# Last layer's hops as float32 64x64 quarter products instead of float32r products over a block matrix

## The reference, cut to what matters

```python
# X = relu(layernorm(x)), [128, 64, 512]; A = adj, [128, 64, 64]
Xw = X @ Wv + bv
sj = Xw @ aw[:d, 0]
si = Xw @ aw[d:, 0]
e = leaky_relu(sj[:, None, :] + si[:, :, None] + ab[0], 0.2)
alpha_matrix = A * exp(e)
transition = alpha_matrix / (sum(alpha_matrix, axis=-1) + 1e-12)
H = 0
Xk = X
for k in range(3):
    H = H + Xk @ Wk[k] + bk[k]
    Xk = einsum('bij,bjd->bid', transition, Xk)
out = x + relu(H)
```

## Time and profile before

| | before |
|---|---|
| median of 3 runs | 2319.44 us |
| lowest and highest | 2314.83 and 2321.06 us |
| span of the profiled execution | 2310.2 us |
| TensorE busy | 2287.1 us (99% of the span) |
| VectorE, ScalarE, GpSimd busy | 57%, 32%, 30% |
| granted TensorE clock, mean | 0.998 |

### The profile page before, as it was taken

One profiled execution on the slowest core, in us unless ns is written; L12 is line 12 of the kernel. 1 busy time (PEld: TensorE's weight loads), 2 busy tenths in 40 slices (PEclk: granted clock), 3 DMA queues, 4 the chain that ended last, 5 costly groups with the idle time before them and its releaser, 6 DMA issues.

```text
span 2310.2 us, 39569 instructions
## 1 busy us (share of the span) xinstructions
PE 2287.1 (99%) x16015; PEld 1860.6 (81%) x16015; DVE 1318.4 (57%) x2745; ACT 747.8 (32%) x1333; POOL 700.2 (30%) x930
## 2 busy tenths in 40 slices
PE   8999999999999999999999999999999999999998
PEld 5788788888878877888888888888778888888887
DVE  3565565656556555545554445555686757676753
ACT  3332323333233333333333333333433232323221
POOL 2433333343333322233322223332342121212120
PEclk9999999999999999999999999999999999999999
DMA  6323333333333343222232222222353333333330
GB/s 198 77 76 95 109 101 83 93 91 87 95 108 105 97 124 105 61 60 67 80 93 60 60 61 60 72 85 95 95 142 94 98 94 97 95 97 96 96 78 37
DMA packets 173479, 209.01 MB, mean 90 GB/s; under 512 B 64800, under 2 KB 81264, under 8 KB 173296
## 3 DMA queue, kind: packets, MB, share of 16 engines
q1 hardware_dynamic: 173296, 206.48, 32.0%
HBM read 88.91 MB, written 50.37 MB: 60 GB/s over the span
## 4 chain that ended last, share of the span: by engine, by line
PE 93%; DVE 2%; SPq 2%; ACT 1%; issue 1%; DMA 1%; POOL 0%; DVEq 0%; ACTq 0%
PE bank L327 50%; PE bank L317 29%; PE bank L588 4%; PE bank L343 3%; SPq L1406 2%; PE bank L528 1%; PE bank L501 1%; PE bank L307 1%; PE bank L378 1%; PE bank L511 1%; PE bank L294 0%; DVE hs L648 0%; DVE yt L961 0%; ACT g1T L1022 0%; PE bank L409 0%
## 5 line engine op out<-in xcount | busy, mean ns | idle before, releaser
L327 PE MATMUL bank<-w_hi,h3T_hi 128*128 128x512 f32 x768 | 302.4, 394 | 0.0
L327 PE MATMUL bank<-w_hi,h3T_lo 128*128 128x512 f32 x768 | 299.5, 390 | 0.0
L327 PE MATMUL bank<-w_lo,h3T_hi 128*128 128x512 f32 x768 | 299.5, 390 | 0.0
L615 DVE TENSOR_TENSOR Z_lo<-bank,Z_hi 128x512 fp32r<-128x512 f32 x128 | 87.1, 682 | 181.6 <-ACT Z_hi L973 181.3
L987 ACT ACTIVATE hn<-x,stA 128x512 f32<-128x512 f32 x192 | 140.7, 804 | 99.3 <-POOL stA L1214 99.3
L327 PEld LDWEIGHTS bank<-w_hi,h3T_hi 128*128 128x128 f32 x768 | 144.6, 188 | 30.2
L327 PEld LDWEIGHTS bank<-w_lo,h3T_hi 128*128 128x128 f32 x768 | 144.4, 188 | 30.2
L327 PEld LDWEIGHTS bank<-w_hi,h3T_lo 128*128 128x128 f32 x768 | 144.4, 188 | 30.2
L973 ACT ACTIVATE Z_hi<-bank 128x512 fp32r<-128x512 f32 x128 | 76.1, 596 | 251.1 <-PE bank L327 159.6
L1209 POOL TENSOR_SCALAR stA<-stA 128x4 f32<-128x4 f32 x48 | 11.5, 241 | 448.1 <-DVE stA L629 446.9
L615 DVE TENSOR_TENSOR cT_lo<-bank,cT_hi 128x256 fp32r<-128x256 f32 x128 | 44.7, 409 | 179.7 <-ACT cT_hi L973 179.7
(11 more groups left out here) (222 smaller groups left out, 5824.9 us busy)
## 6 DMA issues: line engine op xcount, KB each, us to landing
hGA<-hs SPq DMA_DIRECT2D x768, 64.0 KB, 2.0
mid<-x SPq DMA_DIRECT2D x32, 1024.0 KB, 4.8
x<-mid SPq DMA_DIRECT2D x32, 1024.0 KB, 5.8
x<-in_x SPq DMA_DIRECT2D x16, 1024.0 KB, 5.7
hGB<-hs SPq DMA_DIRECT2D x256, 64.0 KB, 2.0
out<-x SPq DMA_DIRECT2D x16, 1024.0 KB, 5.4
blk<-in_adj SPq DMA_DIRECT2D x128, 64.0 KB
adj<-in_adj SPq DMA_DIRECT2D x64, 64.0 KB, 3.3
```

What stands on the lines that cost most here:

```text
L327: ins = eng.matmul(b[:], h[l][:, k, ts], W[r][:, k, :], start=(k == 0 and i == 0), stop=(last and k == 3 and i == 2))
L615: return eng.tensor_tensor(lo, src, hi.bitcast(F), ALU.subtract)
```

## The change

Each hop is made of eight float32 products of a 64x64 matrix by 64x512, in two rounds of four. The four of a round use the four quarters of the array. T is no longer a block matrix with hi and lo parts: GpSimd writes it whole as "own" (a graph's matrix on its own half of the partitions), and ScalarE copies the half that the crossed quarters need to the other half of the partitions ("other"). Z is plain float32; ScalarE copies each bank in two halves of 64 partitions, both to the half of partitions t // 2. VectorE's lo parts of Z and T, GpSimd's four clearings of T, and the tile tt are gone. All four tiles of z1 (and of y) are opened first, and the hops of all four follow behind them; before, each tile had its hop at once. The last group is stored tile by tile. The allocations keep the other tiles' places (pads not shown).

```diff
-        T = [{"hi": alloc(pc, f"Thi{i}", [128, 4, 128], R), "lo": alloc(pc, f"Tlo{i}", [128, 4, 128], R)} for i in range(2)]
+        T = [{"own": alloc(pc, f"Town{i}", [128, 4, 64]), "other": alloc(pc, f"Tother{i}", [128, 2, 64])} for i in range(2)]
...
-            def l3_hop(b, full, g, t, zi):
-                pe.wait_ge(v_tlo, 2 * g + 2)
-                pe.wait_ge(v_zlo[zi], 4 * g + t + 1)
-                for i, (l, r) in enumerate(PASSES):
-                    ins = eng.matmul(b[:], T[g % 2][l][:, t, :], Z[zi][r][:, t, :], start=False, stop=(i == 2))
-                ins.then_inc(full, 1)
+            def l3_hop(zi, name, g):
...
+                pe.wait_ge(a_ts, 2 * g + 2)
+                pe.wait_ge(a_zh[zi], 8 * g + 8)
+                for r in range(2):
+                    for p, c in ((0, 0), (1, 1), (0, 1), (1, 0)):
+                        t = 2 * p + r
+                        b, h = bank.of((name, g, t)), HALF[p]
+                        left = T[g % 2]["own"][h, t, :] if p == c else T[g % 2]["other"][h, r, :]
+                        ins = eng.matmul(b[HALF[c], :], left, Z[zi][h, 2 * r + c, :], start=False, stop=True)
+                        if p != c:
+                            ins.then_inc(bank.done((name, g, t))[0], 1)
...
                 for t in range(4):
-                    b, full, _ = gemm_open(("z1", g, t), hT3[i], t, W3[1], (v_zlo[1], 4 * g + t + 1), False)
-                    l3_hop(b, full, g, t, 0)
+                    gemm_open(("z1", g, t), hT3[i], t, W3[1], (a_zh[1], 8 * g + 2 * t + 2), False)
+                l3_hop(0, "z1", g)
                 pe.wait_ge(p_wlo, lo_pool["w0"])
                 for t in range(4):
-                    b, full, _ = gemm_open(("y", g, t), hT3[i], t, W3[0], (v_y, 4 * g + t + 1), False)
-                    l3_hop(b, full, g, t, 1)
+                    gemm_open(("y", g, t), hT3[i], t, W3[0], (v_y, 4 * g + t + 1), False)
                     if t == 1 + (g == 0) and g + 1 < NG:
                         l3_rowsum(g + 1)
+                l3_hop(1, "y", g)
...
-            def l3_thi(g):
+            def l3_T_other(g):
                 act.wait_ge(p_tt, g + 1)
...
+                for p in range(2):
+                    copy(T[g % 2]["other"][HALF[p], :, :], T[g % 2]["own"][HALF[1 - p], 2 * p:2 * p + 2, :]).then_inc(a_ts, 1)
+
+            def l3_z(zi, key, g, t):
                 act.wait_ge(*bank.done(key))
                 if g:
-                    act.wait_ge(*bank.done((("z1", "y")[zi], g - 1, 3)))
-                copy(Z[zi]["hi"][:, t, :], bank.of(key)[:]).then_inc(a_zhi[zi], 1)
+                    for u in (1, 3):
+                        act.wait_ge(*bank.done((("z1", "y")[zi], g - 1, u)))
+                b = bank.of(key)
+                for c in range(2):
+                    copy(Z[zi][HALF[t // 2], 2 * (t % 2) + c, :], b[HALF[c], :]).then_inc(a_zh[zi], 1)
...
-                    pool.wait_ge(*bank.done(("qk", g, 3)))
-                    for tl in T:
-                        for n in ("hi", "lo"):
-                            eng.memset(tl[n][:].bitcast(F), 0.0).then_inc(p_zero3, 1)
...
+            last = kA(3, NG - 1)
+            for t in range(4):
+                sp.wait_ge(v_x4, 4 * NG - 3 + t)
+                eng.dma_start(out_v[NG - 1][:, t, :], xs[x_slot(last)][:, t, :]).then_inc(d_o[last % 4], 16)
```

More of the change, by code:

```diff
@@ L139, in build @@
             "x_bias q2 k2 z2 zmax zsub zexp2 zrec pn pt vv ct_hi ct_lo x3")
[L141 to L144, removed]
+        (v_dotA, v_sc, v_zc, v_lr, a_ee, p_al, v_rs, p_tt, a_ts, v_y, v_x4) = sems(
+            "dotA scol zc lrelu ee al rs T_own T_other y x4")
+        a_zh = sems("z0_halves z1_halves")
         ident = alloc(root, "ident", [128, 128])
@@ L232, in build @@
         bones = alloc(pc, "bones", [128, 128])
-        tt = alloc(pc, "ttt", [128, 4, 64])
-        alloc(pc, "pad5", [128, 128])
+        alloc(pc, "pad5", [128, 384])
         hT3.append(pair(pc, "h3T1"))
-        Z.append(pair(pc, "Z1"))
+        Z.append(alloc(pc, "Z1", [128, 4, 512]))
+        alloc(pc, "pad9", [128, 2048])
         bkb = alloc(pc, "bkb", [128, 3, 512])
@@ L902, in l3_rowsum @@
                 eng.reciprocal(rs[:], rs[:]).then_inc(v_rs, 1)
[L904 to L911, removed]
-            for g in range(NG):
[L914 to L920, removed]
+            for g in range(NG):
+                if g == 0:
+                    l3_rowsum(0)
+                    l3_sums(dve, eng, 1, (2, 3))
                 if g + 2 < NG:
                     stats_A(3, g + 2)
[L923 to L929, removed]
+                    if g == 0:
+                        adj_T(3, 1)
+                        l3_alpha(1)
+                    transposes(3, g + 2)
                 if g and g + 1 < NG:
@@ L1163, in act_program @@
                         copy(ptc[r][:].rearrange("p m n -> p (m n)"), bank.of(("pT", g, r))[:]).then_inc(a_pt, 1)
-            def l3_thi(g):
+            def l3_T_other(g):
                 act.wait_ge(p_tt, g + 1)
-                act.wait_ge(p_zero3, 4)
                 if g >= 2:
                     act.wait_ge(*bank.done(("y", g - 2, 3)))
-                for h in HALF:
-                    copy(T[g % 2]["hi"][h, :, h], tt[h, :, :]).then_inc(a_thi, 1)
-            def l3_zhi(zi, key, g, t):
+                    act.wait_ge(*bank.done(("y", g - 2, 1)))
+                for p in range(2):
+                    copy(T[g % 2]["other"][HALF[p], :, :], T[g % 2]["own"][HALF[1 - p], 2 * p:2 * p + 2, :]).then_inc(a_ts, 1)
+            def l3_z(zi, key, g, t):
                 act.wait_ge(*bank.done(key))
                 if g:
-                    act.wait_ge(*bank.done((("z1", "y")[zi], g - 1, 3)))
-                copy(Z[zi]["hi"][:, t, :], bank.of(key)[:]).then_inc(a_zhi[zi], 1)
+                    for u in (1, 3):
[3 more added lines that the diff above has]
+                    copy(Z[zi][HALF[t // 2], 2 * (t % 2) + c, :], b[HALF[c], :]).then_inc(a_zh[zi], 1)
             split_in_place(W3[0], d_w0)
@@ L1322, in l3_rowsum @@
                 pool.wait_ge(v_rs, 2 * g + 2)
-                pool.wait_ge(v_tlo, 2 * g)
-                eng.tensor_tensor(tt[:], al[:], rs[:], ALU.mult).then_inc(p_tt, 1)
+                if g >= 2:
+                    pool.wait_ge(*bank.done(("y", g - 2, 3)))
+                    pool.wait_ge(*bank.done(("y", g - 2, 1)))
+                eng.tensor_tensor(T[g % 2]["own"][:], al[:], rs[:], ALU.mult).then_inc(p_tt, 1)
             split_in_place(W3[1], "w1")
@@ L1553, in sp_program @@
                 gather(3, g + 2)
-                sp.wait_ge(v_x4, 4 * g + 4)
-                store_x(kA(3, g), out_v[g])
+                if g + 1 < NG:
+                    sp.wait_ge(v_x4, 4 * g + 4)
+                    store_x(kA(3, g), out_v[g])
+            last = kA(3, NG - 1)
+            for t in range(4):
+                sp.wait_ge(v_x4, 4 * NG - 3 + t)
+                eng.dma_start(out_v[NG - 1][:, t, :], xs[x_slot(last)][:, t, :]).then_inc(d_o[last % 4], 16)
             for i in range(4):
-                sp.wait_ge(d_o[i], 16 * len([k for k in range(3 * NG) if k % 4 == i]))
+                sp.wait_ge(d_o[i], 16 * len([k for k in range(3 * NG) if k % 4 == i]) + (48 if i == last % 4 else 0))
         block = root.enter_context(nc.Block())
```

18 lines of the change are left out of this document (9 added, 9 removed).

## The result

The changed kernel takes 2388.01 us (2387.45 to 2391.89, four runs), the kernel before 2319.03 us (2314.83 to 2321.06, four runs): a ratio of 1.0309 [1.0297, 1.0321], slower. The profiled execution spans 2390.1 us against 2310.2, 79.9 us more; by the medians it is 69.0 us more. The prediction was +41.6, a median of 2361 in a range of 2336 to 2382: the side and the mechanism came, the size did not, and the time lies above the range.

What follows compares the result with a forecast made beforehand. TensorE was taken to set the last layer's pace. Hops -19.8, first hop -4.0, row-sum waits +48.4, clock +14.4, end +2.6 made +41.6 us: span 2351.8, median 2361, range 2336 to 2382.

Steps and rivals of the forecast that it cites:

- Hops: Last layer's hops on TensorE: 2.72 us each before, 2.10 as quarter products; 32 hops save 19.8 us.
- The first hop: TensorE's wait for T's lo part and the low clock behind it both go: 4.0 us saved.
- The place and the cause of the new wait: TensorE stops at the row sum for alpha, because y tiles released together delay the fourth to S+10.8 (S: group's z2 start).
- The size of the wait: At the row sum: exponential at S+31.6, wait 3.5 us, bounds 2.7 (ScalarE's own path) and 4.7; 48.4 us in all.
- the sums' way: SyncE's DMA: 15.2 us from the store to issuing the sums in, landing 4.2 later, at S+30.2.
- Two waits of the fourteen: Row-sum waits by group: none in the first, 3.5 us in groups 1 to 13, 2.9 in group 14.
- The clock: Half clock behind the row-sum waits: nine falls of fourteen at 1.6 us each, 14.4 us; bounds none and 23.8.
- VectorE's and GpSimd's old work: Removing VectorE's lo parts and GpSimd's clearings gives nothing, as TensorE does not wait for them elsewhere.
- The end: From TensorE's last product to the end, last group stored by tiles: 8.9 us instead of 6.25, 2.6 more.
- Span and median: Median of the runs lies 9.2 us above the profiled span, left unchanged: span 2351.8, median 2361.
- Rival 2: Row-sum waits come and the clock falls in each: 2370 us, or 2387 with waits of 4.7; chance 0.22.
- The rule on copies of PSUM: PSUM copies may become the limit; ScalarE takes all Z copies, some 17 us of a 40 us group: delay, not capacity.

Runs made afterwards that it cites:

- experiment 7: Kernel before with its float32r hops behind all four tiles and the row sum behind the fourth y product: 2319.38 us, ratio 1.0021.
- experiment 1: Changed kernel with TensorE's row sum for the next group behind the fourth y product instead of the second: 2292.86 us, ratio 0.9912.
- 6: Changed kernel with the row sum behind the fourth y product and the last group stored whole instead of by tiles: 2297.21 us, ratio 0.9923.
- experiment 3: Kernel before with only its float32r hops moved behind all four tiles of z1 or y: 2414.53 us, ratio 1.0433.
- Experiment 2: Changed kernel with 20 overwritten products of 128x512 ahead of each row sum from group 2's on: 2359.7 us, ratio 1.0199.
- Experiment 4: Changed kernel with VectorE's sums for group g+2 ahead of the y tiles instead of between them: 2357.24 us, ratio 1.0189.
- experiment 5: Changed kernel with the row sum behind the fourth y product and four GpSimd clearings into unused memory put back: 2291.64 us, ratio 0.9907.
- experiment 8: Changed kernel, VectorE's g+2 sums first, VectorE copying z1 tiles 2 and 3 and making alpha before its transposes, norm_A later: 2300.62 us, ratio 0.994.

## Why the prediction was right in kind and short in size

**Hops, right.** Predicted 0.62 us each, 19.8 in all. The timeline gives 2.72 - 2.09 = 0.63, the spans of experiments 7 and 1 give 18.8 for all hops, the medians of 7 and 6 up to 23.

**The first hop, right.** The wait for the lo part of T, 2.3 us, is gone, and with it the low clock behind it.

**The place and the cause of the new wait, right.** It stands at the row sum and waits for alpha; experiment 1 removes it by one line, experiment 3 makes it with the old form. The delay starts where the prediction put it, with four y tiles that come free at once and the fourth done at S+10.8. So the change of placement is what makes the kernel slower, and not the quarters, which are a gain.

**The size of the wait, the first term that failed.** The step was: "The exponential starts at about S+31.6 ... a wait of 3.5 us." In groups 2 to 13 it came at S+33.0 on average and the waits were 3.5 to 6.2, 4.8 on average. The term that was mis-sized is the sums' way: out and back in were put at 15.2 us from the store to the issue of the sums in and 4.2 for their landing, from one group of before and a median; in the group read they took 16.0 and 4.6, and the median landing of the changed kernel is 4.9. The path through x and ScalarE was well sized: the last copy ends at S+30.7 to S+31.5, where the prediction had S+31.7.

One group was thin ground for such a term: in groups 2 to 13 of the kernel before, the time from the issue of the sums out to that of the sums in goes from 10.1 to 13.6 us (11.0 on average, 10.8 in the group taken). In the changed kernel the same step takes 11.5 us on average, in experiments 1 and 2 it takes 10.7 and the landing 4.2, and there the exponential starts at S+31.5 and S+31.7. So the prediction's sum came true for this chain in two of its neighbours; in the changed kernel the sums' way is some 1.4 us longer. Why, is open: that TensorE stops in every group is not enough, since in experiment 3, where it does too, the step takes 10.6 and the landing 4.1. Experiment 4 takes the sums off the path and leaves 2.9 us, near the floor of 2.7.

**Two waits of the fourteen were wrong.** Group 1 was put down like the rest and had 8.5 us: its x was issued at 1734.96 and its first statistics came only 14.5 us later:

```profile
1749.48 0.69 DVE L637 BATCH_NORM_STATS2 stA<-x 128x6 f32<-128x512 f32 x1 [13.49 <-DMA x<-mid]
```

Group 14 had 0.9 instead of 2.9, and group 0, put at nothing, had 0.8. In sum 67.5 us stand against 48.4: 19 us of the shortfall, of which the twelve groups with 4.8 instead of 3.5 make 15. What held up group 1's load was not found. The gathers issued just ahead of it do not explain it: in the kernel before they end 2.1 us ahead of this group's store (here 5.1) and the statistics start 9.1 us behind the store (here 14.9), and here the DMA engines move nothing any more in the last 5 us ahead of them:

```profile
1745.00:1750.00 5.00, 5.00 (x30) 2.86 (x29) 0.52 (x1) 2.37 (x4) 0.00 (x0) 1.00 0.00 0
```

Experiments 1 and 2 have the same delay (13.1 and 13.6 us), experiment 4 does not (8.4).

**The clock, the second term that failed.** The step was: "I take nine of fourteen, at 1.6 us each." All 13 long waits were followed by the lower level, at 2.26 us in the group read and 2.4 on average, 31 us together, against 14.4. The average comes from the distance of the row sums: twelve groups, from 1761.62 to 2296.97, take 535.35 us; a group of experiment 1, without a wait, takes 37.27 (1984.87 to 2022.14), twelve of them 447.2; the twelve waits take 57.3 and 12 x 0.16 more; 28.9 are left. Experiment 2 has 25 to 30 for its twelve. Both parts of the term were short, the count (nine instead of 13) and the price (1.6 instead of 2.4). The page TensorE: Matmul & The Clock Gate of the Trainium skill (HAM oscillation) describes a loop that goes cold in every pass because TensorE waits in every pass; here the trace agrees, 13 of 13. The size of one fall was taken from a single window of before in which the low clock lasted 3.4 us; here it lasted from the row sum at 2072.66 to 2077.09.

**VectorE's and GpSimd's old work.** "VectorE's lo parts and GpSimd's clearings cost nothing today and give nothing" was wrong in one place: without the clearings the wait for VV is 2.1 us longer, since GpSimd's h3T_lo then lies beside the steps that make VV (experiment 5).

**The end.** 8.9 us were predicted behind TensorE's last product and 7.1 came: the landing of 256 KB was taken at 4.2 us, the sums' time, and takes 2.0. Before it was 6.25: 0.85 more instead of 2.6.

**Span and median.** The prediction left 9.2 us between them as they were. It was no constant, and what the device does around the instructions is 1.8 us of it at most: the profiled execution of the changed kernel took 2391.89 us, 1.8 above its span, and so it is in every execution on record that lists its span (1.75 to 1.87). The rest was the spread between executions. The prediction of the median was 7 us too high for that, which hid a part of the miss: 38.3 us by the spans (2351.8 to 2390.1), 27 by the medians (2361 to 2388.0).

The account of the span: hops -19.8, first hop -4.0, waits at the row sum +67.5 and 15 x 0.16 = +2.4, clock +31.2 (13 x 2.4), VV +2.1, end +0.85. That makes +80.3; +79.9 was measured.

Rival 2, falls in each wait with waits of 4.7, had 2387 and came within 1 us. Its mechanism was right; that it came so near is in part luck, as its falls at 1.7 us each were 7 us short in sum and the 9.2 us for the median 7 too many.

The rule on copies of PSUM, weighed in the prediction, is borne out in part at most: the page TensorEngine Tiling (Array Packing) of the Trainium skill, under PSUM Bottleneck, wants ScalarE and VectorE to share them, and in experiment 8, where they do, the wait is gone, but VectorE's order was changed along with it. And it is delay that is cured, not a lack of capacity; one later line for the row sum does the same.

**Open.** Two things were not found: why the sums' write and their read back landed later in the changed kernel (11.5 and 4.9 us) than in experiments 1 and 2 (10.7 and 4.2), and why single groups stray (10.6 to 12.3 us for the write in groups 2 to 13). The changed kernel was traced in one execution only. In the group read it is not traffic at the end: the write, issued at 2053.73, has not landed at 2065, and from 2060 to 2065 the DMA engines move nothing. DMA traffic was not changed by itself in any run.

## What to carry to other kernels

Ask of a batched step not only what it costs but what it now releases at once: four tiles that came free one by one and now come together put a store, a load and a chain over four engines 8 us later, and a consumer that had 1.7 us of cover waits 3.5 to 6.2. Take the time of a DMA round trip from many groups, with its spread, and not from one, and count a clock fall for every wait of that length that a loop repeats; here 31 us of clock came on top of 67 us of waits. And before a form is blamed or given up, move the waiting instruction: one line turned +3.1% into -0.9%.

## What the runs showed of the hardware

- Float32 products of 64x64 in four quarters: eight of 512 columns, four at a time, cost 2.09 us, the change to quarters and back included; twelve float32r products of 128x512 cost 2.72.
- A copy from PSUM of 64x512 takes ScalarE 0.592 us, one of 128x512 0.58 to 0.60.
- Waits of TensorE of 2.9 us were followed by the lower clock level in 11 of 13 cases (experiment 4), those of 3.5 to 8.5 us in all 13 (after), those of up to 1.4 us in none of five (experiment 7). One fall cost 2.4 us on average (after). A wait of 1.5 us for h1T_lo in layer 1 was followed by it in one run (experiment 4) and not in before.
- GpSimd's float32 work on 128x512 beside VectorE slowed a VectorE instruction on 128x512 from 0.68 to 1.74 us and a tiny one from 0.51 to 1.10, and took 5.78 us itself instead of 4.98 (after and experiment 5).
- Useless products in the waits brought 28.3 us by the medians (2388.0 to 2359.7), 25 to 27 of them by keeping the clock up.
- The write of the sums to DRAM and the wait for it took 8.9 us in the one group in which no x is loaded ahead of it (group 14), 10.6 to 12.3 in groups 2 to 13 (after).
